# Layer 0: the reciprocal by seed and Newton steps with operands in PSUM banks, and three products as fp16 passes

## The reference, cut to what matters

```python
xn = _layernorm(x)
# layer 0, attention branch
xs = pad(xn)[:, :-1]
xm = xn * time_mix + xs * (1.0 - time_mix)
k = einsum('btc,dc->bdt', xm, Wk)
v = einsum('btc,dc->bdt', xm, Wv)
r = einsum('btc,dc->btd', xm, Wr)
k = exp(minimum(k, 60.0)); kv = k * v
wkv = causal_conv(kv, w)                 # w: decay per channel
wk = causal_conv(k, w) + 1e-09
s = (sigmoid(r) * swapaxes(wkv / wk, 1, 2)) @ Wo.T
# layer 0, gate branch: three layers of +-1 weights, 128 -> 512 -> 512 -> 128
g = silu(_L0_ffn_ref(xn, ...))
x = x + s * g
# layer 1: a selective scan and a mixture of experts, the same outer form
```

## Time and profile before

| | us |
|---|---|
| median of 3 runs | 672.55 |
| lowest, highest | 672.5, 673.92 |
| the profiled execution's own time | 672.1 |
| its span, first to last instruction | 670.3 |
| granted TensorE clock, share of full speed | 0.997 |

### The profile page before, as it was taken

The page is one execution under the profiler, slowest core; times in us unless marked ns, Lnnn a source line. Parts: engine busy times, 40 slices in busy tenths (PEclk is TensorE's granted clock), DMA queues, the critical chain, the costliest instruction groups (busy, mean ns, idle before and its releaser), DMA issues. The chain is left out here.

```text
span 670.3 us, 9285 instructions
## 1 busy us (share of the span) xinstructions
PE 629.5 (94%) x2714; PEld 304.2 (45%) x2714; DVE 601.0 (90%) x1406; ACT 511.4 (76%) x794; POOL 280.1 (42%) x275
## 2 busy tenths in 40 slices
PE   4779999999999998799999999999999999999986
PEld 2334444444444443344545444454444544444442
DVE  4999999999999999988988988898898899889856
ACT  2846666666666665889988898898888889899886
POOL 6556777777777765222123032122313303221220
PEclk9999999999999999999999999999999999999999
DMA  7331000000000000000000000000000000000000
GB/s 178 109 94 31 1 0 1 1 0 1 0 2 1 0 1 1 1 0 1 16 1 17 17 4 14 16 17 0 17 17 1 17 17 17 0 18 17 0 17 32
DMA packets 10770, 11.65 MB, mean 17 GB/s; under 512 B 4800, under 2 KB 6288, under 8 KB 10720
## 3 DMA queue, kind: packets, MB, share of 16 engines
q1 hardware_dynamic: 9744, 10.73, 5.3%
q0 software_dynamic: 112, 0.33, 0.1%
q10 hardware_dynamic: 864, 0.00, 0.1%
HBM read 6.87 MB, written 4.19 MB: 16 GB/s over the span
## 5 line engine op out<-in xcount | busy, mean ns | idle before, releaser
L1150 PE MATMUL bank<-arena,w 128*128 128x512 f16 x640 | 148.6, 379 | 4.1 <-DVE arena L774 4.1
L1150 PE MATMUL bank<-arena,dnT 128*128 128x512 f32 x288 | 138.6, 592 | 0.0
L435 POOL TENSOR_TENSOR arena<-arena 128x512 f32<-128x512 f32 x48 | 59.7, 1271 | 137.6 <-ACT arena L590 137.6
L650 ACT ACTIVATE arena<-bank,xinv 128x512 f32<-128x512 f32 x144 | 94.4, 693 | 24.9 <-PE bank L1150 24.6
L1150 PEld LDWEIGHTS bank<-arena,w 128*128 128x128 f16 x640 | 62.5, 98 | 78.3 <-issue 10.1
L482 ACT ACTIVATE arena<-bank 128x512 f16<-128x512 f32 x96 | 53.8, 606 | 35.8 <-PE bank L1150 35.8
L425 POOL TENSOR_TENSOR arena<-arena 128x512 f32<-128x512 f32 x16 | 16.8, 1050 | 140.6 <-DVE arena L1011 140.6
L1150 PEld LDWEIGHTS bank<-arena,dnT 128*128 128x128 f32 x288 | 53.7, 191 | 35.9 <-issue 24.4
L1150 PE MATMUL bank<-arena,wsqT 128*128 128x512 f32 x128 | 64.6, 609 | 5.3 <-DVE arena L783 5.3
L1020 DVE SCALAR_TENSOR_TENSOR arena<-bank,cws,arena 128x506 f32<-128x506 f32 (+1 forms) x96 | 67.1, 740 | 1.1
L774 DVE SCALAR_TENSOR_TENSOR arena<-bank,arena 128x512 f16<-128x512 f32 x96 | 60.3, 671 | 2.4 <-ACT arena L482 1.2
(11 more groups left out here) (221 smaller groups left out, 1492.6 us busy)
## 6 DMA issues: line engine op xcount, KB each, us to landing
x_all<-in_L_attn_x SPq DMA_DIRECT2D x16, 256.0 KB, 2.6
out<-x_all SPq DMA_DIRECT2D x16, 256.0 KB, 2.0
up_n<-in_L_ffn_routed_up SPq DMA_DIRECT2D x1, 512.0 KB, 3.7
dn_n<-in_L_ffn_routed_down SPq DMA_DIRECT2D x1, 512.0 KB, 5.3
wx<-in_L_attn_W_x SPq DMA_DIRECT2D x1, 288.0 KB, 2.9
k_u<-in_L_ffn_k POOLq DMA_DIRECT2D x1, 256.0 KB, 5.8
w_in<-in_L_attn_W_in SPq DMA_DIRECT2D x1, 256.0 KB, 2.7
k_u<-in_L_ffn_k SPq DMA_DIRECT2D x1, 128.0 KB, 6.1
```

Of the source, the lines that this page charges most:

```text
L435: g.tensor_tensor(prod[:, c, :], act[:, c + 1, :], gate[:, :], ALU.mult).then_inc(sem["b_actp"], 1)
L650: a.activation(act[:, c, :], up_bank(f, c)[:, :], ACT.Gelu, scale=xinv[:, I_UP:I_UP + 1]).then_inc(sem["b_act"], 1)
L1150: return nc.tensor.matmul(ps, lhsT, rhs, start=start, stop=stop)
```

## The change

From group 2 on, k, v and r are made from fp16 halves. ScalarE writes `xmh`, the fp16 copy of the mixed rows, VectorE `xml`, what is left, and each product is three fp16 passes: high weights by high rows, low weights by high rows, high weights by low rows. The halves of the weights (`sqH`, `sqL`) are made once, in `scales`, with one more column in the table of magnitudes; groups 0 and 1 keep the fp32 products (`plain`). The mixed rows now carry a factor of 2**11, which the readers of the three products take out (`unscale`, `half_sq`). Exp of k is written back to its bank, and the minimum reads it there.

The reciprocal of `wk` is no longer VectorE's `reciprocal`. ScalarE reads `wk` as integers and makes a seed with one Exp, and copies `wk` to bank `b_F`. VectorE then does a product (`b_S` = `rec` * `b_F`), a step (`rec` = (`b_S` - 2.00045) * `rec`, which has the sign turned), a second product, and a second step that is merged with the product with `ysr`: GpSimd multiplies `ysr` by the once improved `rec` (`a_q`), and VectorE's second step gives `ya`. The sign is turned back in `sg` by a factor of -0.5. Further, TensorE does hidden piece 1 ahead of turning `sg` back, and VectorE does the value scans behind `gp`.

The core of the diff:

```diff
+LOG2 = math.log(2.0)
+SEED_SCALE = -LOG2 / 2 ** 23
+SEED_BIAS = LOG2 * (127 - 0.043)
+NEWTON = 2.00045
...
+        def plain(n):
+            return isinstance(n, int) and n < 2
+        def unscale(n):
+            return 1.0 / XS if plain(n) else xinv[:, I_SQ:I_SQ + 1]
...
-                    pool.wait_ge(sem["a_rec"], m + 1)
+                if has(m):
+                    pool.wait_ge(sem["a_r1"], m + 1)
                     pool.wait_ge(sem["a_ysr"], m + 1)
-                    after(pool, sem["a_s"], m)
-                    g.tensor_tensor(ya[:, :], ysr[:, :], rec[:, :], ALU.mult).then_inc(sem["a_y"], 1)
+                    g.tensor_tensor(ysr[:, :], ysr[:, :], rec[:, :], ALU.mult).then_inc(sem["a_q"], 1)
...
+                    if not plain(f):
+                        actv.wait_ge(sem["a_xm"], f + 1)
+                        after(actv, sem["a_r"], f)
+                        a.activation(xmh[:, :], xm[:, :], ACT.Copy).then_inc(sem["a_xmh"], 1)
+                if has(m):
+                    actv.wait_ge(sem["a_wk"], m + 1)
+                    after(actv, sem["a_q"], m)
+                    a.activation(rec[:, :], wk[:, :].bitcast(mybir.dt.int32), ACT.Exp, scale=SEED_SCALE,
+                                 bias=seedb[:, :]).then_inc(sem["a_rec"], 1)
+                    after(actv, sem["a_gp"], m)
+                    a.activation(b_F[:, :], wk[:, :], ACT.Copy).then_inc(sem["a_wkp"], 1)
...
-                    a.activation(ek[:, :], b_K[:, :], ACT.Exp).then_inc(sem["a_ek"], 1)
+                    a.activation(b_K[:, :], b_K[:, :], ACT.Exp, scale=unscale(f)).then_inc(sem["a_ek"], 1)
...
+            def first_product(n):
+                dve.wait_ge(sem["a_rec"], n + 1)
+                dve.wait_ge(sem["a_wkp"], n + 1)
+                after(dve, sem["a_sg"], n)
+                v.tensor_tensor(b_S[:, :], rec[:, :], b_F[:, :], ALU.mult).then_inc(sem["a_t1"], 1)
+            def first_step(n):
+                dve.wait_ge(sem["a_t1"], n + 1)
+                v.scalar_tensor_tensor(rec[:, :], b_S[:, :], NEWTON, rec[:, :], ALU.subtract, ALU.mult).then_inc(sem["a_r1"], 1)
+            def second_product(n):
+                dve.wait_ge(sem["a_r1"], n + 1)
+                v.tensor_tensor(b_S[:, :], rec[:, :], b_F[:, :], ALU.mult).then_inc(sem["a_t2"], 1)
+            def second_step(n):
+                dve.wait_ge(sem["a_t2"], n + 1)
+                dve.wait_ge(sem["a_q"], n + 1)
+                after(dve, sem["a_s"], n)
+                v.scalar_tensor_tensor(ya[:, :], b_S[:, :], 2.0, ysr[:, :], ALU.add, ALU.mult).then_inc(sem["a_y"], 1)
...
+                    if not plain(f):
+                        dve.wait_ge(sem["a_xmh"], f - 1)
+                        after(dve, sem["a_r"], f)
+                        v.tensor_tensor(xml[:, :], xm[:, :], xmh[:, :], ALU.subtract).then_inc(sem["a_xml"], 1)
...
-                    dve.wait_ge(sem["a_wk"], m + 1)
-                    after(dve, sem["a_y"], m)
-                    v.reciprocal(rec[:, 0:N // 2], wk[:, 0:N // 2])
+                    first_product(m)
+                    first_step(m)
+                    second_product(m)
...
-                    v.tensor_scalar(ekm[:, :], ek[:, :], math.exp(K_CAP), None, ALU.min).then_inc(sem["a_ekm"], 1)
+                    v.tensor_scalar(ekm[:, :], b_K[:, :], math.exp(K_CAP), None, ALU.min).then_inc(sem["a_ekm"], 1)
                     dve.wait_ge(sem["a_ekm"], f + 1)
                     dve.wait_ge(sem["a_v"], f + 1)
                     after(dve, sem["a_kvc"], f)
-                    v.tensor_tensor(kv[:, :], ekm[:, :], b_V[:, :], ALU.mult).then_inc(sem["a_kv"], 1)
+                    v.scalar_tensor_tensor(kv[:, :], b_V[:, :], unscale(f), ekm[:, :], ALU.mult, ALU.mult).then_inc(sem["a_kv"], 1)
+                if has(m):
+                    second_step(m)
...
-                    v.reciprocal(rec[:, N // 2:], wk[:, N // 2:]).then_inc(sem["a_rec"], 1)
                     low(1, m, 2)
                     low(1, m, 3)
...
+                if has(f) and f != 0:
+                    low(0, f, 0)
+                    low(0, f, 1)
+                    low(0, f, 2)
+                    low(0, f, 3)
+                if has(m):
+                    dve.wait_ge(sem["a_thf"], m + 1)
+                    after(dve, sem["a_sg"], m)
+                    v.scalar_tensor_tensor(gp[:, :], thf[:, :], 1.0, b_F[:, :], ALU.add, ALU.mult).then_inc(sem["a_gp"], 1)
                 if has(f):
                     dve.wait_ge(sem["a_kv"], f + 1)
                     after(dve, sem["a_wkv"], f)
                         last = v.tensor_tensor_scan(Pv[:, s, 1:], dec[:, :], kv[:, s * T:(s + 1) * T], 0.0,
                                                     ALU.mult, ALU.add)
                     last.then_inc(sem["a_scanV"], 1)
-                if has(f) and f != 0:
-                    low(0, f, 0)
-                    low(0, f, 1)
-                    low(0, f, 2)
-                    low(0, f, 3)
-                if has(m):
-                    dve.wait_ge(sem["a_thf"], m + 1)
-                    after(dve, sem["a_sg"], m)
-                    v.scalar_tensor_tensor(gp[:, :], thf[:, :], 1.0, b_F[:, :], ALU.add, ALU.mult).then_inc(sem["a_gp"], 1)
+                if has(m):
                     dve.wait_ge(sem["a_gp"], m + 1)
                     dve.wait_ge(sem["a_s"], m + 1)
                     after(dve, sem["a_sgT"], m)
-                    v.scalar_tensor_tensor(sg[:, :], b_S[:, :], c3[:, 2:3], gp[:, :], ALU.mult, ALU.mult).then_inc(sem["a_sg"], 1)
+                    v.scalar_tensor_tensor(sg[:, :], b_S[:, :], c3[:, 3:4], gp[:, :], ALU.mult, ALU.mult).then_inc(sem["a_sg"], 1)
...
+                v.tensor_scalar(half_sq[:, :], col(xinv, I_SQ), 0.5, None, ALU.mult)
+                halves(sqH[:, :], sqL[:, :], wsqT[:, 0:3, :].rearrange(flat), col(wsc, I_SQ)).then_inc(sem["sq_ready"], 1)
...
+                def square(ps, i):
+                    if plain(f):
+                        return mm(ps[:, :], wsqT[:, i, :], xm[:, :])
+                    w = slice(i * P, (i + 1) * P)
+                    if i == 0:
+                        pe.wait_ge(sem["sq_ready"], 1)
+                        pe.wait_ge(sem["a_xmh"], f - 1)
+                    mm(ps[:, :], sqH[:, w], xmh[:, :], True, False)
+                    mm(ps[:, :], sqL[:, w], xmh[:, :], False, False)
+                    if i == 0:
+                        pe.wait_ge(sem["a_xml"], f - 1)
+                    return mm(ps[:, :], sqH[:, w], xml[:, :], False, True)
```

95 lines of the change are left out of this document (58 added, 37 removed).

## The result

| | before | after |
|---|---|---|
| median of 4 runs, us | 673.23 | 686.74 |
| after / before, 95% interval | | 1.0196 (1.0174 to 1.0217) |
| span of the profiled execution, us | 670.3 | 685.2 |
| `xm` to `xm`, groups 3 to 14, us | 15.52 | 16.20 |

The account below looks back on a forecast made before the run. A ring through nearly all of VectorE was taken as the bound: 14.80 + 0.45 + 1.25 = 16.50 us a group, 16.42 by starts. With once-only terms +12.0, so 672.55 + 12.0 = 684.5 us, range 668 to 690 (8 in 10).

Parts of the forecast that it names:

- VectorE's sum without holds, 14.80: Steady group: VectorE's instructions, reciprocals swapped for Newton steps plus `xml`, sum to 14.80 us instead of 15.52 if nothing waits.
- TensorE's 0.64 less is worth nothing: Steady group: fp16 passes take 0.64 us off TensorE, which then needs some 14.1 us and doesn't set the period.
- ScalarE's order sets when GpSimd's product comes: Steady group: three new ScalarE instructions delay the relus, so GpSimd's product ends at 7.39 and the second step waits 0.45.
- `xml` held by `ysr`: Steady group: `xml`, with two SBUF operands, is held by GpSimd's `ysr`, cost 0.45 us, making it over 1 us long.
- The key scans overtaken: Steady group: GpSimd's centring holds the first key scan and its scaling goes in before the second; cost 1.25 us.
- Rival B: Steady group: GpSimd's scaling doesn't overtake the second scan; period 15.57, kernel 673.5 us; chance 0.12.
- Rival C: Steady group: scans and `xml` not held, GpSimd's product ending before 5.6; 669.3 us, down to 663; chance 0.18.
- Rival D: Steady group: seed and bank copy take 1.0 each instead of 0.6, ring 0.8 longer; 695 us; chance 0.08.
- The set-up, +1.7: Once: a magnitude over 384 columns and scaled halves of three matrices on VectorE, at most 0.6 each; +1.7 us.
- Groups 2 to 14, +11.7: Thirteen layer 0 groups with the new passes, each 0.90 us longer (16.42 for 15.52); +11.7 us.
- The turn to layer 1, -1.0: Last group's tail: reciprocals to layer 1's first turned rows loses one reciprocal's half, then waits on ScalarE; -1.0 us (0 to -1.6).
- The end, 0: Layer 1 itself: unchanged, so no difference in time.

Follow-up runs that it names:

- Run 11: The changed kernel with the seed ahead of `prev` on ScalarE and GpSimd's scaling of normalised rows waiting for both key scans; 675.42 us, 1.0040 to before.
- Run 2: The kernel before with the fp16 passes alone, hardware reciprocal and old order kept; 676.79 us, 1.0051 to before, period 15.69 us.
- Run 3: The changed kernel with ScalarE's order alone changed: seed ahead of `prev`, copy of `wk` ahead of `xmh`; 677.21 us, 1.0065 to before, period 15.53.
- run 5: The changed kernel with one wait more: GpSimd's scaling of the normalised rows waits for both key scans; 676.96 us, 1.0062 to before, period 15.40.
- run 9: The changed kernel; in the last group, GpSimd takes the root for layer 1's first rows before its product with the receptance; 687.95 us, 1.0216 to before.
- Run 8: The changed kernel without ScalarE's copy of `wk` to the bank, so both Newton products read two SBUF operands; 694.13 us, 1.0331 to before.
- run 4: The changed kernel with the key scans reading their data from a PSUM bank, one SBUF operand instead of two; 673.08 us, 1.0014 to before.
- run 6: The changed kernel with fp32 keys, values and receptance throughout, their fp16 set-up removed, and GpSimd's scaling waiting for both key scans; 668.46 us, 0.9925 to before.
- run 12: Run 10 with GpSimd's low halves and product in the last group waiting until layer 1's normalised rows are done; 660.80 us, 0.9804 to before.
- run 10: Run 6 with the chain of scales cut into pieces ahead of later groups' key scans, layer 1's input-matrix halves included; 661.64 us, 0.9824 to before.

## Why the prediction was right, step by step

- **VectorE's sum without holds, 14.80.** The steps with a bank as destination were taken at 0.69 and took 0.67 to 0.70. Run 11, whose scans are free and whose `xml` is held 0.6, has 15.27; less some 0.55 this is 14.7. The sum holds within 0.1.
- **TensorE's 0.64 less is worth nothing.** Run 2 shows it: 0.17 slower. TensorE's longest gap in the changed kernel's steady group (0.86) is ended by the low halves, as forecast.
- **ScalarE's order sets when GpSimd's product comes.** The first relu comes 2.43 after `xm` (2.47 forecast), the seed takes 0.71 and the copy 0.58, the product ends at 7.28 (7.39), the second step starts at 7.49 (7.43). Run 3 confirms that the place of these instructions matters, not their cost.
- **`xml` held by `ysr`.** Forecast 0.45 and over 1 us long; 1.23, ending 0.55 behind `ysr`.
- **The key scans overtaken.** Forecast 1.0 to 1.1 and 1.5 us, cost 1.25, and 0.85 of it by the scaling between the scans; the trace has 0.82 and 1.46, 2.19 for the pair, 0.93 over the free 1.26. The first scan was oversized by 0.2: it starts 9.28 after `xm`, and the centring ends 0.16 sooner than laid out. The price of the scaling was right: run 5 gives 0.80. This term's 0.32 is more than the whole difference between 16.42 and 16.20.
- **Rival B** (second scan not overtaken, 15.57) needed another order on GpSimd: made by a wait in run 5, it gives 15.40. **Rival C** (no holds) asked for the product to end before 5.6 after `xm`; no run brought it that far; in run 3 it ends at 6.21, and of the 0.93 of the scans' hold 0.26 was left. **Rival D** (dear seed or copy) fell by their rows.
- **The set-up, +1.7, measured +2.98: undersized.** What the term names cost 1.5: the reduce 0.44 from start to start, the halves and their factor 1.05. GpSimd's holds are no part of the rest. The changed kernel has a single-column addition at 1.22 and a product of 8x8 numbers (L939) at 1.17, some 2.0 too long together; but the kernel before has a single-column product at 1.05, value scans at 2.06 and key scans at 1.42 in the same group, some 1.9 too long. What the term left out is TensorE's clock in groups 0 and 1. The six fp32 matmuls of group 0 took 5.21 for 4.54, at the start, before the clock had risen. In run 9, with the same code up to there, they took 4.88, so this part differs from one execution to the next. In group 1 four took 3.56 for 1.98, and VectorE waited 1.23 for ScalarE in front of its low halves, where it had not waited before; its key scans come 9.08 after `xm` for 8.36. Run 8 has the same wait of TensorE's there (2.70), but full clock behind it (1.98 again); VectorE doesn't wait, and the scans come at 8.20.
- **Groups 2 to 14, +11.7, measured +9.64.** The steady difference is 0.68 where 0.90 was forecast. Group 2 alone gives 1.50, more than twice as much, with TensorE at the lower clock for some 5 us of it. That the clock would fall in layer 0 was named only as a sign of being wrong at the root. It did fall, but in groups 1 and 2 alone; the steady groups ran at full clock, and their holds are as laid out.
- **The turn to layer 1, -1.0, measured +2.33: the wrong sign.** The step that failed reads "the step from the reciprocals to the first turned rows of layer 1 loses one reciprocal's half and waits on ScalarE then". Ahead of those rows VectorE doesn't wait on ScalarE: w_inH took 1.20 for 0.46 behind `ysr`, the normalised rows 3.43 for 2.13 beside GpSimd's low halves and its new product. A reciprocal had filled a part of that time before, and isn't held. TensorE waited 2.98 for 1.03 and ran at the lower clock behind it (eight matmuls in 2.74 for 1.89). Runs 3, 4, 6, 8 and 11 have the same rows of 3.43 and the same wait, and full clock behind it: this stretch is 20.25 to 20.27 there. So some 1.5 of the 2.33 are the holds, and 0.8 the clock. It is the same rule that the prediction applied in the steady group, and did not in the tail. That run 9's remedy failed and run 12's held shows that it was GpSimd's low halves and its product; no run parts the two.
- **The end, 0, measured +0.94.** Two stretches at the lower clock make it up. In the changed kernel the last distance between two `sg` is 18.71 for 17.02; the windows of the last 30.3 us have a granted clock of 0.94 there and 1.00 before. In the kernel before it is the first distance of layer 1 that is longer, 37.66 for 37.00. The code is the same in both, and why the clock falls in one place or the other isn't settled; for the last 30.3 us run 12 has 0.94 too, and run 10 0.99.

The errors of these terms cancel in part: groups 2 to 14 were 2.1 too dear, the rest 5.0 too cheap. The whole came out 2.2 us above the forecast, inside its range. That it came so near is in part luck; the steady group's waits and their order are not.

## What to carry to other kernels

Before VectorE gets faster or longer at one place, list which of its instructions take two operands (or a fast mode) from SBUF, and what GpSimd does at their new times; a pair of back-to-back ones pays a whole GpSimd instruction if one waits. Such holds show in no idle time: compare the length of the same instruction in two places. They go by an operand in a bank, by order, or by one wait on GpSimd more; try these before judging a change by its first time. And work taken off an engine that isn't the bound has to pay for what it adds elsewhere: here the fp16 passes added 1.32 us a group to the kernel with Newton steps, and saved nothing.
